# A decoder layer on one core: the second norm's variance moved to ScalarE, gates and bias blocks to GpSimd

## The reference, cut to what matters

```
y1 = ln(x + mha(x)) * g1 + be1
gates = softmax(xf @ wg);  idx = argmax(gates);  keep = loc < cap
out = where(keep, gate_val * y[slot], 0)          # y = (x @ w1 + b1) @ w2 + b2 of the chosen expert
y2 = ln(y1 + out) * g2 + be2,   ln(x) = (x - mu) * rsqrt(mean((x - mu)**2) + eps)
```

## Time and profile before

| what | value |
|---|---|
| median of three runs | 338.67 us (338.23 to 341.26) |
| profiled execution | 339.11 us, span of its instructions 337.3 us |
| TensorE busy | 319.2 us, 95% of the span |
| VectorE busy | 261.2 us, 77% |
| ScalarE busy | 166.6 us, 49% |
| GpSimd busy | 126.0 us, 37% |

### The profile page before, as it was taken

One profiled execution on the slowest core, in us unless ns is written; L12 is line 12 of the kernel. 1 busy time (PEld: TensorE's weight loads), 2 busy tenths in 40 slices (PEclk: granted clock), 3 DMA queues, 4 the chain that ended last, 5 costly groups with the idle time before them and its releaser, 6 DMA issues.

```text
span 337.3 us, 12339 instructions
## 1 busy us (share of the span) xinstructions
PE 319.2 (95%) x4780; PEld 219.0 (65%) x4780; DVE 261.2 (77%) x661; ACT 166.6 (49%) x458; POOL 126.0 (37%) x208
## 2 busy tenths in 40 slices
PE   7869999999999999999999999999999999998994
PEld 3425556666666556565565665657666769898994
DVE  6874578866667789998899999875555638879996
ACT  2223545666666446455465564645425546733331
POOL 1063555100000254645423534234700005814896
PEclk9976999999999999999999999999999999999998
DMA  4972230636456163589556000000000000044412
GB/s 109 300 201 87 70 138 25 181 113 150 144 166 163 50 177 90 157 194 226 163 145 193 3 4 2 2 6 1 2 2 4 2 2 0 6 126 132 152 30 66
DMA packets 38697, 31.89 MB, mean 95 GB/s; under 512 B 4968, under 2 KB 36208, under 8 KB 38512
## 3 DMA queue, kind: packets, MB, share of 16 engines
q1 hardware_dynamic: 36064, 27.37, 28.9%
q0 software_dynamic: 1280, 3.15, 3.8%
q10 hardware_dynamic: 1296, 0.59, 0.7%
HBM read 23.40 MB, written 7.70 MB: 92 GB/s over the span
## 4 chain that ended last, share of the span: by engine, by line
PE 73%; DVE 10%; issue 8%; POOL 5%; ACT 1%; DMA 1%; POOLq 0%; DVEq 0%
PE ps L1328 9%; PE ps L1311 9%; PE ps L1274 8%; PE ps L1248 3%; PE ps L1227 3%; PE ps L1284 3%; PE ps L1361 3%; PE ps L1240 3%; PE ps L1399 3%; PE ps L1698 2%; PE ps L1344 2%; PE ps L1417 2%; PE ps L1218 2%; PE ps L1437 2%; POOL room L913 2%
## 5 line engine op out<-in xcount | busy, mean ns | idle before, releaser
L969 ACT ACTIVATE pT<-ps 128x512 f32<-128x512 f32 x128 | 73.9, 612 | 89.4 <-PE ps L1284 81.8
L837 POOL TENSOR_TENSOR rstd<-veps,minus_half 128x1 f32<-128x1 f32 x32 | 18.8, 586 | 117.2 <-DVE veps L452 117.1
L487 DVE TENSOR_REDUCE m_pad<-ps 128x8 f32<-128x1024 f32 x32 | 39.1, 1222 | 19.4 <-PE ps L1311 19.2
L463 DVE TENSOR_TENSOR p_sb<-qk_sb,heads 128x512 f32<-128x512 f32 x64 | 45.0, 705 | 0.9 <-ACT qk_sb L984 0.5
L490 DVE TENSOR_REDUCE m_pad<-ps 128x8 f32<-128x1024 f32 x32 | 38.9, 1216 | 0.0
L1274 PE MATMUL ps<-p_sb,qk_sb 32*128 32x512 f32 x256 | 38.1, 667 | 0.0
L1311 PE MATMUL ps<-p_sb,qk_sb 32*128 32x512 f32 x256 | 37.5, 656 | 0.0
L1328 PE MATMUL ps<-pT,p_sb 128*32 128x128 f32 x1024 | 35.1, 276 | 0.2 <-issue 0.2
L1284 PE MATMUL ps<-mT,negsel 32*128 32x128 f32 x512 | 33.0, 365 | 0.4 <-issue 0.4
L1698 PE MATMUL ps<-mexp,pT 128*128 128x128 f32 x256 | 31.9, 278 | 1.2 <-DVE pT L784 0.9
L1284 PEld LDWEIGHTS ps<-mT,negsel 32*128 32x128 f32 x512 | 21.3, 192 | 16.2 <-issue 16.2
(11 more groups left out here) (203 smaller groups left out, 682.0 us busy)
## 6 DMA issues: line engine op xcount, KB each, us to landing
room<-mask_rows SPq DMA_DIRECT2D x32, 128.0 KB, 3.4
wkv_sb<-wkv SPq DMA_DIRECT2D x23, 128.0 KB
kv_sorted<-room SPq DMA_DIRECT2D x5, 512.0 KB, 3.1
w1t_sb<-w1t SPq DMA_DIRECT2D x8, 256.0 KB
w_sb<-w SPq DMA_DIRECT2D x8, 256.0 KB
kv_sb<-hot_rows SPq DMA_DIRECT2D x4, 512.0 KB, 5.4
ctx_sorted<-room SPq DMA_DIRECT2D x1, 1472.0 KB, 10.3
tk<-fside SPq DMA_DIRECT2D x1, 1024.0 KB
```

Source lines behind the costliest of these rows:

```text
L463: return dve.tensor_tensor(dst, rows.unsqueeze(1).broadcast_to([128, QUADS, S]), heads[:, 0, :].unsqueeze(2).broadcast_to([128, QUADS, S]) ...
L487: dve.tensor_reduce(m4[:, 0:2, 0:QUADS], ps[:, 0:2, :].rearrange("p g (j k) -> p g j k", j=QUADS), AX.X, ALU.max).then_inc(s["max_low"], 1)
L837: pool.tensor_tensor(rstd[:, :], veps[:, :], minus_half[:, :], ALU.pow)\
L969: act.activation(pT[:, t % 2, g, :, :], quad[4 + g], ACT.Exp).then_inc(s["exped"], 1)
```

## The change

- `cblk` blocks 8 to 15 are made on GpSimd by `tensor_scalar`, 8 to 11 ahead of the first half's gates and 12 to 15 behind them. Each waits for the block before, the first for ScalarE's eighth.
- `route_gates(0)` leaves VectorE. One operation stays there (room times pick, `room_known`); the sums over eight experts, the reciprocal (a power of -1) and the last product are eight dependent operations on GpSimd (`first_gates`), a sum of eight being three halvings. `route_gates` of the second half stays on VectorE with two operations made one.
- For batches 0 to 11 of the second norm, line 810 writes the row sums too (`accum_out`), ScalarE makes sum - 128 z (`less_rows`) and a new `row_squares` squares these, with the sum over the row, and VectorE scales that into `ve16` (`squares_variance`, one batch after the pair). `bn_stats` and `bn_aggr` remain for batches 12 to 15.
- The load of `w_out` signals `xw_in` instead of `attn_w_in`, and `route_picks` waits for `y1_ready` 1 instead of `picks_clear`.

```diff
+            def squares_variance(b):
+                dve.wait_ge(s["squared"], b + 1)
+                dve.tensor_scalar(ve16[:, b - 1:b + 1], zsquares[:, b - 1:b + 1], float(D), EPS * D * D, ALU.mult, ALU.add)\
+                    .then_inc(s["ve_ready"], 1)
...
-            def route_gates(h):
+            def route_gates():
...
-                route(dve.tensor_scalar(r_b[:, n, :], batches(bank[6 + h]), float(CAP), None, ALU.is_lt))
-                route(dve.tensor_tensor(r_b[:, n, :], r_b[:, n, :], pick_bf[:, h, n, :], ALU.mult))
+                route(dve.scalar_tensor_tensor(r_b[:, n, :], batches(bank[7]), float(CAP), pick_bf[:, 1, n, :],
+                                               ALU.is_lt, ALU.mult))
...
                 if m == 1:
-                    route_gates(0)
+                    dve.wait_ge(s["place_done"], 1)
+                    dve.scalar_tensor_tensor(r_b[:, half(0), :], batches(bank[6]), float(CAP), pick_bf[:, 0, half(0), :],
+                                             ALU.is_lt, ALU.mult).then_inc(s["room_known"], 1)
...
+                    if b < B - 4:
+                        dve.scalar_tensor_tensor(z16[:, b, :], bank[4 + b % 2][:, 0:D], gate[:, b:b + 1], y1[:, b, :],
+                                                 ALU.mult, ALU.add, accum_out=zsum[:, b:b + 1]).then_inc(s["z_ready"], 1)
+                    else:
...
-                    if b % 2 and b < B - 2:
+                    if b % 2 == 0 and 2 <= b <= B - 4:
+                        squares_variance(b - 1)
+                    if b == B - 3:
                         pair_variance(b, 1)
...
-            for b in range(B - 6, B):
+            def bias_block(b):
+                pool.wait_ge(s["cblk_ready"], max(b, B // 2))
+                pool.tensor_scalar(cblk[:, b, :], crep[:, :], batchof[:, b:b + 1], None, ALU.mult)\
+                    .then_inc(s["cblk_ready"], 1)
+            def gate_step(ins, step):
+                ins.then_inc(s["gate_step"], 1)
+                pool.wait_ge(s["gate_step"], step)
+            def first_gates():
+                n = half(0)
+                pool.wait_ge(s["gexp_ready"], 1)
+                halves = lg[:, n, :]
+                gate_step(pool.tensor_tensor(halves[:, :, 0:4], halves[:, :, 0:4], halves[:, :, 4:8], ALU.add), 2)
+                gate_step(pool.tensor_tensor(halves[:, :, 0:2], halves[:, :, 0:2], halves[:, :, 2:4], ALU.add), 3)
+                gate_step(pool.tensor_tensor(gate[:, n], halves[:, :, 0], halves[:, :, 1], ALU.add), 4)
+                gate_step(pool.tensor_tensor(gate[:, n], gate[:, n], minus_one[:, :], ALU.pow), 5)
+                pool.wait_ge(s["room_known"], 1)
+                room_left = r_b[:, n, :]
...
+                pool.tensor_tensor(gate[:, n], gate[:, n], r_s[:, n], ALU.mult).then_inc(s["gate_ready"], 1)
+            gate_step(pool.memset(minus_one[:, :], -1.0), 1)
+            for b in range(B - 6, B - 2):
                 y1_row(b)
+            for b in range(B // 2, B - 4):
+                bias_block(b)
+            first_gates()
+            for b in range(B - 2, B):
+                y1_row(b)
+            for b in range(B - 4, B):
+                bias_block(b)
...
             def less_rows(b):
-                act.wait_ge(s["mv_step"], 2 * B + 2 * (b // 2) + 2)
-                act.activation(z16[:, b, :], z16[:, b, :], ACT.Identity, scale=-1.0, bias=mv16[:, b, 0:1])\
+                act.wait_ge(s["z_ready"], b + 1)
+                act.activation(z16[:, b, :], z16[:, b, :], ACT.Identity, scale=-float(D), bias=zsum[:, b:b + 1])\
...
+            def row_squares(b):
+                act.wait_ge(s["c_ready"], b + 1)
+                if b >= 2:
+                    act.wait_ge(s["squared"], b - 1)
+                act.activation(offs[:, b % 2, :], z16[:, b, :], ACT.Square, scale=1.0 / D, accum_out=zsquares[:, b:b + 1])\
+                   .then_inc(s["squared"], 1)
...
-            for b in range(8, B):
-                bias_block(b)
             turned_picks(1)
...
                     less_rows(b)
+                for b in (2 * i, 2 * i + 1):
+                    row_squares(b)
```

More of the change, by code:

```diff
@@ L171, in decoder_kernel @@
         ve16 = sb("ve16", [128, B])
+        zsum = sb("zsum", [128, B])
+        zsquares = sb("zsquares", [128, B])
+        offs = sb("offs", [128, 2, D])
+        minus_one = sb("minus_one", [128, B // 2])
         half16 = sb("half16", [128, B])
@@ L210, in decoder_kernel @@
             f_exped f_den_done f_ln_done f_rden_ready f_pv_done aT_ready f_proj_done z_ready w_ready y1_ready
-            y1T_done y1T_copied logits_done route_step shifted gexp_ready pick_ready gate_ready place_done
-            pickT_done pickT_copied picks_clear cblk_ready y1_rooted c_ready u_ready out_step last_rows pair_summed pair_rows hot_out hot_in_2 hot_in_3 hot_in_4 hot_in_5 hot_in_6 hot_in_7 xb_ready hot_done gated ffn_done out_rows""".split()
+            y1T_done y1T_copied logits_done route_step shifted gexp_ready pick_ready gate_ready room_known gate_step place_done
+            pickT_done pickT_copied cblk_ready y1_rooted c_ready squared u_ready out_step last_rows pair_summed pair_rows hot_out hot_in_2 hot_in_3 hot_in_4 hot_in_5 hot_in_6 hot_in_7 xb_ready hot_done gated ffn_done out_rows""".split()
         assert len(names) == len(set(names))
@@ L281, in _ @@
             sp.dma_start(x_sb[:, 4:B, :], x[4:B].rearrange("b s d -> s b d")).then_inc(s["x_rest_in"], 16)
-            sp.dma_start(w_out_sb[:, 0, :], w_out).then_inc(s["attn_w_in"], 16)
+            sp.dma_start(w_out_sb[:, 0, :], w_out).then_inc(s["xw_in"], 16)
             def bucket_weights(i):
@@ L757, in route_picks @@
                 route(dve.tensor_reduce(r_m[:, n], r_b[:, n, :], AX.X, ALU.max))
-                dve.wait_ge(s["picks_clear"], 1)
+                dve.wait_ge(s["y1_ready"], 1)
                 dve.tensor_tensor(pick_bf[:, h, n, :], r_b[:, n, :], bcast(r_m[:, n]), ALU.is_equal)\
                    .then_inc(s["pick_ready"], 1)
-            def route_gates(h):
-                n = half(h)
-                dve.wait_ge(s["gexp_ready"], h + 1)
+            def route_gates():
+                n = half(1)
+                dve.wait_ge(s["gexp_ready"], 2)
                 route(dve.tensor_reduce(r_s[:, n], lg[:, n, :], AX.X, ALU.add))
                 route(dve.reciprocal(gate[:, n], r_s[:, n]))
-                dve.wait_ge(s["place_done"], h + 1)
-                route(dve.tensor_scalar(r_b[:, n, :], batches(bank[6 + h]), float(CAP), None, ALU.is_lt))
-                route(dve.tensor_tensor(r_b[:, n, :], r_b[:, n, :], pick_bf[:, h, n, :], ALU.mult))
+                dve.wait_ge(s["place_done"], 2)
+                route(dve.scalar_tensor_tensor(r_b[:, n, :], batches(bank[7]), float(CAP), pick_bf[:, 1, n, :],
+                                               ALU.is_lt, ALU.mult))
                 route(dve.tensor_reduce(r_s[:, n], r_b[:, n, :], AX.X, ALU.add))
@@ L809, in _ @@
                     dve.wait_ge(s["y1_ready"], b + 1)
-                    dve.scalar_tensor_tensor(z16[:, b, :], bank[4 + b % 2][:, 0:D], gate[:, b:b + 1], y1[:, b, :],
-                                             ALU.mult, ALU.add).then_inc(s["z_ready"], 1)
-                    z_stats(b, 1)
-                    if b % 2 and b < B - 2:
+                    if b < B - 4:
+                        dve.scalar_tensor_tensor(z16[:, b, :], bank[4 + b % 2][:, 0:D], gate[:, b:b + 1], y1[:, b, :],
+                                                 ALU.mult, ALU.add, accum_out=zsum[:, b:b + 1]).then_inc(s["z_ready"], 1)
+                    else:
+                        dve.scalar_tensor_tensor(z16[:, b, :], bank[4 + b % 2][:, 0:D], gate[:, b:b + 1], y1[:, b, :],
+                                                 ALU.mult, ALU.add).then_inc(s["z_ready"], 1)
+                        z_stats(b, 1)
+                    if b % 2 == 0 and 2 <= b <= B - 4:
+                        squares_variance(b - 1)
+                    if b == B - 3:
                         pair_variance(b, 1)
@@ L821, in _ @@
                 if m == 5:
-                    route_gates(1)
+                    route_gates()
             last_variance(B - 1)
@@ L862, in add_bo @@
                 if t == B:
-                    pool.wait_ge(s["xw_in"], 48)
+                    pool.wait_ge(s["xw_in"], 64)
                 pool.wait_ge(s["xn_ready"], t + 1)
@@ L916, in out_row @@
                     .then_inc(s["out_rows"], 1)
-            pool.memset(pick_bf[:, :, :, :], 0.0).then_inc(s["picks_clear"], 1)
+            pool.memset(pick_bf[:, :, :, :], 0.0)
             def y1_row(b):
@@ L1354, in project_out @@
                 if t == 0:
-                    pe.wait_ge(s["attn_w_in"], 16)
+                    pe.wait_ge(s["xw_in"], 16)
                 if t == B:
-                    pe.wait_ge(s["xw_in"], 48)
+                    pe.wait_ge(s["xw_in"], 64)
                 pe.wait_ge(s["exped"], min(4 * t + 14, 4 * T))
```

17 lines of the change are left out of this document (10 added, 7 removed).

## The result

The changed kernel is slower: 345.38 us, median of six runs, against 338.24 us for the kernel before in the same rounds, a ratio of 1.023 (95% interval 1.0186 to 1.0275). An execution can also fall into a slower state of the chip, and the ratios here are of executions outside it, so that they aren't quite the quotients of the medians (here 1.021). The forecast was 346.5 against 338.67, also a ratio of 1.023. The profiled execution has a span of 345.3 us against 337.3.

What follows compares the result with a forecast made beforehand. TensorE was taken as the bound, 73% of the last chain, so changes act through what it waits for or behind its last product. +4.0 + 2.2 + 0.8 + 0 + 0.9 = +7.9 us on 338.67 gave 346.5 us, range 340 to 351.

Steps and rivals of the forecast that it cites:

- Part 1: Before ffn(2): first half's gates on GpSimd behind four bias blocks make ffn(2) late, +4.0 us (+1.5 to +6.2).
- Part 3, first pass: Between ffn(2) and ffn(6): VectorE waits for ScalarE's first squares, ffn(6) later by +0.8 us (-1.0 to +1.3).
- Part 2: Behind the gap before ffn(2): TensorE's clock falls to half for 4 to 5 us, +2.2 us (0 to +3.4).
- (a): Rival at the gap before ffn(2): TensorE's clock stays up, 344.4 us; chance 0.18.
- (c): Rival: GpSimd's forms at lower bounds, gap of 1.5 to 2 us spares the clock, VectorE's relief shows, 339.7 us; chance 0.13.
- Part 3, ten batches: From ffn(6) to the end of ffn(15): squares loop and GpSimd's work leave no gain, 0 us (-1.0 to +1.0).
- Part 4: Behind TensorE's last product: GpSimd's last power at +3.0 us, last output row later, +0.9 us (0 to +1.4).
- (e): Rival in the second norm: squares relieve nobody since GpSimd paces pairs in both kernels; counted within the forecast, no own chance.
- (d): Rival between the batches: TensorE waits for VectorE's queue, freeing it gives nearly 3.0 us, 336.7 us; chance 0.07.
- (b): Rival: GpSimd as slow as its 0.525 us row, or ScalarE loop over 4.4 us, some 350.5 us; chance 0.17.

Runs made afterwards that it cites:

- e1: The changed kernel with first_gates ahead of bias blocks 8 to 11 on GpSimd instead of behind them; ratio 1.008 to the kernel before.
- e6: The kernel before with only the first half's gates on GpSimd and two operations of the second half's gates made one; ratio 0.9996.
- e7: The kernel before with only bias blocks 8 to 15 on GpSimd and room times pick one operation in both halves' gates; ratio 0.9995.
- e2: The changed kernel with twenty unused products on TensorE in the gap before ffn(2); ffn(2) to ffn(6) 2.24 us shorter, 10.30 us.
- e4: The kernel before with the squares variance alone, room times pick merged in both halves; +0.30 us before ffn(6), +0.07 in the ten batches, +0.98 at the end.
- e5: e1 with squares_variance of a pair one batch later on VectorE; ratio 1.0043 to the kernel before.
- e9: e4 with ScalarE's offsets and squares ahead of the previous pair's roots, the first pair's ahead of the turned picks; ratio 1.0033 to the kernel before.
- e11: e9 with the product with the norm's gain moved from GpSimd to VectorE, a pair at once; ratio 0.9899 to the kernel before.

## Why the prediction was right

The sum, +7.9 us, was right because its terms were, within 0.8 us each; the stage took +8.5. A part of the closeness is luck: part 1 was 0.8 us too small and the first pass of part 3 0.5 too large.

- **Part 1** (+4.0, bounds 1.5 to 6.2): measured 7.97 - 3.16 = +4.81. The mechanism is as told, and e1, e6 and e7 show that it is the order and neither the gates nor the blocks. Mis-sized was the block: 0.60 us and 0.10 to the next, at the upper bound of 0.60, where I had taken 0.45 and 0.08 of semaphore time, so the four took 2.7 us instead of 2.1. The gates took 3.77 us (300.75 to 304.52) against 3.8: the small operations were 0.28 to 0.34 from start to start and the power 1.67 against 1.4. The Trainium skill's page GPSIMD Engine Reference (§ 3.1) had led to an estimate of 0.2 for a small operation; here they are 0.20 to 0.25.
- **Part 2** (+2.2): 2.24 by e2. Rival (a), that the clock stays up, is out. The prediction called the 3.14 us gap the only comparable one, but the trace of the kernel before has a second slow stretch: behind idle times of 0.71 and 0.85 us with one short group of products between them, the clock was 0.50 in the window below. That spoke against (a), and against (c), in which a gap of 1.5 to 2 us leaves the clock alone.

```profile
15.03 0.30 PE L1210 MATMUL ps<-ident,m_pad 128*128 128x128 f32 x1 [0.71 <-issue]
16.18 0.44 PE L1240 MATMUL ps<-causal,ident_bf 32*32 32x512 bf16 x16 [0.85 <-DVE p_sb L463]
...
18.00:20.00 2.00, 2.00 (x28) 0.87 (x12) 1.76 (x5) 0.00 (x0) 1.02 (x1) 0.50 1.04 264
```

- **Part 3, first pass** (+0.8): +0.30 with a full clock. Up to `ffn(5)` it came as told: in e4 VectorE went on 6.13 us behind `ffn(2)` (told 6.4) and `ffn(5)` began at 7.81 (told 7.85). What was too dear is what followed: the update with its sum took 0.27 us from start to start where I had taken 0.5, 0.15 of it for the sum, and the five gate operations 1.09 instead of 1.25. The accumulator's read is there as an instruction, as the page VectorE: DVE Perf Modes of the Trainium skill (§ Two Vector instructions with no wait between them) has it, but no time is seen for it: the next operation started 0.28 us behind line 824's start. VectorE stood longer than told, 2.28 to 2.59 us instead of 1.8, since it came to the wait sooner.
- **Part 3, ten batches** (0): +0.09 in the changed kernel. The prediction named two bounds at once, the loop through ScalarE and GpSimd's own work, and they act on different things. e5 and e9 show that the loop held TensorE (20.4 us without it), and e9 to e11 that GpSimd's work is a second bound right behind, which holds the end.
- **Part 4** (+0.9): 6.49 - 5.43 = +1.06, with the last power at +2.98 (told: +3.0). e4 has it with part 3 alone, so it is part 3's. Rival (e), that GpSimd paces the pairs in both kernels, holds for the end, in the kernel before too (e9), and not for TensorE's batches.

Rivals (c) and (d) needed the gates 3 to 4 us sooner; no block or gate was at its lower bound. Of (b) one half came true, the block at 0.60 us was slower than its 0.525 us row; the small operations were not, and so part 1 stayed at 4.81 and did not reach 6.2.

## What to carry to other kernels

Work moved to an idle engine is as cheap as its place in that engine's queue: look for what the first moved operation waits for, and for who waits behind the last one, before its price. The same two moves cost nothing alone and 6.5 us in the wrong order. A gap that is made on TensorE can be paid again in its clock, 2.24 us here, and filling it with idle products is a test of that price. And relief of one engine shows only when the next one has room. GpSimd was busy for 37% of the span and yet without a pause in the last 21 us of its work; what the relief of VectorE gave could be seen only when work was taken off GpSimd too.

## What was not expected of the hardware

- A `tensor_scalar` of 128x128 f32 with a column as scalar took 0.60 us on GpSimd with VectorE idle, more than a two-input operation of that size (0.46). From start to start it was 0.70, over twice ScalarE's 0.30.
- GpSimd's power took 1.67 us for eight columns, 0.70 for two: 0.16 a column.
- An output row of 0.46 us on GpSimd took 1.4 to 1.5 us when it met a gating operation on VectorE with both inputs in SBUF (322.36 in e9, behind VectorE's row at 322.21, and 324.24). The page SBUF — State Buffer of the Trainium skill (§ Who interferes with whom) says that such a VectorE instruction contends with a GpSimd instruction that reads SBUF; these rows agree.
- An accumulator output cost nothing visible on VectorE (0.08 us, overlapped). On ScalarE a square with its sum was issued 0.30 us behind the one before (312.74 and 313.04 in the changed kernel), as was a bias block without a sum (2.44 us for eight).
